# Rounding of the hidden activations moved from ScalarE to VectorE, w2 load issue moved, and the two weight quantisations merged, in a pre-norm transformer block with a ternary-weight FFN

## The reference

```python
def act_quant(x):
    scale = 127.0 / jnp.clip(jnp.max(jnp.abs(x), axis=-1, keepdims=True), 1e-05)
    return jnp.clip(jnp.round(x * scale), -128, 127) / scale
def weight_quant(w):
    scale = 1.0 / jnp.clip(jnp.mean(jnp.abs(w)), 1e-05)
    return jnp.clip(jnp.round(w * scale), -1, 1) / scale
# bit_linear(x, w) = act_quant(x) @ weight_quant(w).T
h = bit_linear(x, w1)                      # 1024 -> 4096
h = depthwise_conv1d(h, conv_w, conv_b)    # 3 taps along the sequence
h = silu(h)
return bit_linear(h, w2)                   # 4096 -> 1024
x = x + attn(layernorm(x)); x = x + ffn(layernorm(x))
```

## Time and profile before

| | us |
|---|---|
| time, median of 2 runs | 4887.63 (4877.98 to 4897.29) |
| the profiled execution | 4897.44 |
| its span on the slowest core (core 2) | 4895.9 |
| spans of the eight cores | 4848.8 to 4895.9 |
| PE busy | 2891.8 (59%) |
| DVE busy | 1615.2 (33%) |
| ACT busy | 1370.4 (28%) |

### The profile page before, as it was taken

One profiled execution on the slowest core, in us unless ns is written; L12 is line 12 of the kernel. 1 busy time (PEld: TensorE's weight loads), 2 busy tenths in 40 slices (PEclk: granted clock), 3 DMA queues, 4 the chain that ended last, 5 costly groups with the idle time before them and its releaser, 6 DMA issues. The chain is left out here.

```text
span 4895.9 us, 49561 instructions; the slowest of 8 cores (4848.8 to 4895.9 us)
## 1 busy us (share of the span) xinstructions
PE 2891.8 (59%) x17394; PEld 1464.8 (30%) x17576; DVE 1615.2 (33%) x3705; ACT 1370.4 (28%) x1640; POOL 45.5 (1%) x68
## 2 busy tenths in 40 slices
PE   0166557778411156767675466467778266677775
PEld 0022123334211134434341122133434143343341
DVE  1121143322233555443432212232111554443431
ACT  0011024457211223232313011024656223140412
POOL 0000000000000000000000000000000000000000
PEclk9999756665655578989777799666565698877878
DMA  7400022111435023435343300000000034434334
GB/s 135 154 22 18 17 95 78 61 61 44 110 97 187 28 53 90 134 105 149 95 125 114 118 22 13 18 27 14 5 18 1 9 69 103 143 101 124 109 108 140
DMA packets 472113, 380.93 MB, mean 78 GB/s; under 512 B 340674, under 2 KB 373570, under 8 KB 466756
## 3 DMA queue, kind: packets, MB, share of 16 engines
q1 hardware_dynamic: 460612, 335.81, 24.2%
q0 software_dynamic: 11264, 41.95, 2.6%
HBM read 335.77 MB, written 41.94 MB: 77 GB/s over the span
## 5 line engine op out<-in xcount | busy, mean ns | idle before, releaser
L80 ACT ACTIVATE b_pt<-b_lp,b_cb 128x1024 bf16<-128x1024 f32 (+3 forms) x640 | 621.4, 985 | 557.0 <-PE b_lp L80 354.8
L80 PE MATMUL c_op<-c_w2b,c_hq 128*128 128x512 bf16 x2032 | 578.8, 435 | 306.6 <-DMA c_w2b<-w2t_s 125.7
L80 PE MATMUL c_hp<-c_xq,c_w1b 128*128 128x257 bf16 x4096 | 550.7, 293 | 117.2 <-ACT c_H L80 108.5
L80 PEld LDWEIGHTS c_hp<-c_xq,c_w1b 128*128 128x128 bf16 x4096 | 420.4, 104 | 285.4 <-issue 192.5
L80 PE MATMUL b_av<-V,b_pt 128*128 128x65 bf16 x5120 | 377.4, 237 | 207.0 <-ACT b_pt L80 146.5
L80 PEld LDWEIGHTS b_av<-V,b_pt 128*128 128x128 bf16 x5120 | 297.0, 124 | 422.0 <-issue 421.9
L80 ACT ACTIVATE c_H<-c_hp,c_cb 128x512 bf16<-128x512 f32 x256 | 175.0, 684 | 824.4 <-DVE c_H L80 531.3
L80 PEld LDWEIGHTS c_op<-c_w2b,c_hq 128*128 128x128 bf16 x2048 | 209.1, 107 | 648.4 <-issue 522.4
L80 PE MATMUL b_lp<-Q,K 64*128 64x512 bf16 x1280 | 371.0, 591 | 11.0 <-DVE x L80 9.3
L80 DVE TENSOR_TENSOR c_H<-c_hp,c_g1b 128x514 bf16<-128x514 f32 x256 | 177.0, 691 | 578.1 <-PE c_hp L80 578.1
L80 DVE MEMSET b_pt<- 128x256 bf16 (+2 forms) x192 | 93.1, 485 | 622.8 <-PE b_lp L80 570.5
(11 more groups left out here) (125 smaller groups left out, 2451.0 us busy)
## 6 DMA issues: line engine op xcount, KB each, us to landing
c_w2b<-w2t_s SPq DMA_DIRECT2D x256, 512.0 KB, 5.4
c_w1b<-w1t_s SPq DMA_DIRECT2D x128, 512.0 KB, 4.6
pw_stg<-w SPq DMA_DIRECT2D x32, 1024.0 KB, 4.9
wq_stw<-w SPq DMA_DIRECT2D x16, 2048.0 KB, 9.0
a_xt<-x SPq DMA_DIRECT2D x32, 512.0 KB, 3.5
b_xr<-x SPq DMA_DIRECT2D x32, 512.0 KB, 3.6
out<-c_obf POOLq DMA_DIRECT2D x32, 512.0 KB, 3.0
wq_s<-p_wbf POOLq DMA_DIRECT2D x16, 512.0 KB, 7.3
```

The source lines that it names most:

```text
L80: h = getattr(eng, en["name"])(*en["args"], **en["kwargs"])
```

## The change

It has four parts.

1. `wprep_quant` becomes `wprep_quant_all`: one loop over 16 blocks, 8 of w1 and then 8 of w2, through the same buffers. The barrier between the two weights is gone, and so is the fresh start of the pipeline.
2. `emit_hq_batch`: both additions of the rounding constant are one DVE `tensor_scalar` (two additions, from c_t, out as bfloat16) instead of two ACT activations. DVE drains after each pair of multiplies and each pair of roundings. Waits on ACT go; PE waits for DVE instead of ACT before a w2 sub; the SiLU into Hb2 waits for the rounding and no longer for the multiply; in front of the batch between tiles it is DVE that waits for the last w2 sub of the previous tile.
3. The batch of a group is recorded earlier: behind the first w2 sub of the group and before w1 chunk 2g+1, where it stood behind `emit_mx`.
4. The w2 load is recorded inside `emit_w2_sub`, right before the sub, where both loads stood at the head of the group.

```diff
-            for blk in range(8):
-                par = blk % 2
+            for j16 in range(16):
+                which = "w1" if j16 < 8 else "w2"
+                t_w = t_w1 if j16 < 8 else t_w2
+                sw_bc = sw1_bc if j16 < 8 else sw2_bc
+                blk = j16 % 8
+                par = j16 % 2
...
-            wprep_quant(t_w1, sw1_bc, mw1_bc, "w1")
-            wprep_quant(t_w2, sw2_bc, mw2_bc, "w2")
+            wprep_quant_all()
...
             def emit_w2_sub(t, half, glob):
                 vp = 0 if half == 0 else 2
                 wb2 = glob % 2
                 g2c = 2 * glob
+                r.wait(r.sync, tn, w2b_cons[wb2])
+                dlw = dw2[wb2].inc(r.sync.dma_start(
...
-                r.wait(r.tensor, sc, ve_hq[2 * glob + 1])
-                r.wait(r.tensor, dw2[wb2], dl_w2[wb2])
+                r.wait(r.tensor, ve, ve_hq[2 * glob + 1])
+                r.wait(r.tensor, dw2[wb2], dlw)
...
-                r.wait(r.scalar, ve, ve_hqm[hc])
+                r.wait(r.scalar, ve, ve_hq[hc])
...
                 r.wait(r.vector, sc, sc_sil[c0 + 3])
-                r.wait(r.vector, sc, ve_hq[(c0 + 31) % 32])
                 for pair in range(2):
-                    if pair == 1:
-                        r.wait(r.vector, sc, ve_hq[c0 + 1])
-                    mv_h = 0
                     for k in range(2):
                         c = c0 + 2 * pair + k
-                        mv_h = ve.inc(r.vector.tensor_mul(
+                        ve.inc(r.vector.tensor_mul(
                             ct1[:, k * 512:(k + 1) * 512],
                             Hb2[:, c * 512:(c + 1) * 512], S2sb[:, :]))
-                        ve_hqm[c] = mv_h
-                    r.wait(r.scalar, ve, mv_h)
+                    ve.inc(r.vector.drain())
                     for k in range(2):
                         c = c0 + 2 * pair + k
-                        sc.inc(r.scalar.activation(
-                            ct1[:, k * 512:(k + 1) * 512],
-                            ct1[:, k * 512:(k + 1) * 512],
-                            AF.Identity, bias=magic_bc[:, 0:1]))
-                    sc.inc(r.scalar.drain())
-                    for k in range(2):
-                        c = c0 + 2 * pair + k
-                        ve_hq[c] = sc.inc(r.scalar.activation(
+                        ve_hq[c] = ve.inc(r.vector.tensor_scalar(
                             hqg[:, c * 512:(c + 1) * 512],
                             ct1[:, k * 512:(k + 1) * 512],
-                            AF.Identity, bias=nmagic_bc[:, 0:1]))
+                            MAGIC, -MAGIC, ALU.add, ALU.add))
+                    ve.inc(r.vector.drain())
...
-                    if w2t is not None:
-                        emit_w2_load(2 * (g % 8))
-                        emit_w2_load(2 * (g % 8) + 1)
                     dg_build(2 * g + 1)
...
                     if w2t is not None:
                         emit_w2_sub(w2t, g // 8, 2 * (g % 8))
+                        if g <= 6:
+                            emit_hq_batch(w2t, 4 * (g + 1))
                     w1_chunk(2 * g + 1, sl)
...
-                    if w2t is not None and g <= 6:
-                        emit_hq_batch(w2t, 4 * (g + 1))
...
                 if t > 0:
-                    r.wait(r.scalar, tn, w2_done[t - 1])
+                    r.wait(r.vector, tn, w2_done[t - 1])
                 emit_hq_batch(t, 0)
```

More of the change, by code:

```diff
@@ L248, in build_program, with wprep_quant_all @@
         r.emit()
[L250 to L256, removed]
+    def wprep_quant_all():
+        with nc.sbuf_tensor("wq_st", [128, 2 * 4096], F32) as stg2, \
+             nc.sbuf_tensor("wq_f", [128, 4096], F32) as qf, \
+             nc.sbuf_tensor("wq_b", [128, 4096], BF16) as qb8, \
+             nc.sbuf_tensor("wq_sp", [128, 4096], BF16) as strip, \
+             nc.psum_tensor("wq_tp", [128, 1024], BF16) as tpp:
             ve_q = 0
@@ L260, in wprep_quant @@
             sc_q = [0, 0]
-            for blk in range(8):
-                par = blk % 2
+            for j16 in range(16):
[4 more added lines that the diff above has]
+                par = j16 % 2
                 stg = stg2[:, par * 4096:(par + 1) * 4096]
-                if blk >= 2:
+                if j16 >= 2:
                     r.wait(r.sync, sc, sc_q[par])
                 if which == "w1":
-                    src = t_w.rearrange("(hc p) (fc f) -> fc p hc f",
-                                        p=128, f=128)[blk]
+                    src_w = t_w.rearrange("(hc p) (fc f) -> fc p hc f",
+                                          p=128, f=128)[blk]
                     dlx[par].inc(r.sync.dma_start(
                         out=stg.rearrange("p (hc f) -> p hc f", hc=32),
-                        in_=src), 16)
+                        in_=src_w), 16)
                 else:
-                    src = t_w.rearrange("(oc p) (hg hq) -> hg p oc hq",
-                                        p=128, hq=512)[blk]
+                    src_w = t_w.rearrange("(oc p) (hg hq) -> hg p oc hq",
+                                          p=128, hq=512)[blk]
                     dlx[par].inc(r.sync.dma_start(
                         out=stg.rearrange("p (oc hq) -> p oc hq", oc=8),
-                        in_=src), 16)
+                        in_=src_w), 16)
                 r.wait(r.scalar, dlx[par])
-                if blk > 0:
+                if j16 > 0:
                     r.wait(r.scalar, ve, ve_q)
@@ L292, in wprep_quant @@
                 for g in range(4):
-                    if not (blk == 0 and g == 0):
+                    if not (j16 == 0 and g == 0):
                         r.wait(r.tensor, ve, ve_g)
@@ L296, in wprep_quant @@
                         if which == "w1":
-                            src_t = qb8[:, (g * 8 + k) * 128:(g * 8 + k + 1) * 128]
+                            src_t = qb8[:, (g * 8 + k) * 128:
+                                        (g * 8 + k + 1) * 128]
                         else:
@@ L947, in build_program @@
             ve_hq = [0] * 32
-            ve_hqm = [0] * 32
             tn_cv = [0] * 32
@@ L960, in build_program @@
             w2b_cons = [0, 0]
[L962 to L971, removed]
             def emit_w2_sub(t, half, glob):
@@ L976, in emit_w2_sub @@
                 g2c = 2 * glob
+                r.wait(r.sync, tn, w2b_cons[wb2])
+                dlw = dw2[wb2].inc(r.sync.dma_start(
+                    out=w2b[:, wb2 * 2048:(wb2 + 1) * 2048].rearrange(
+                        "p (l m) -> p l m", l=2),
+                    in_=t_w2t[g2c:g2c + 2].rearrange("l p m -> p l m")), 16)
                 if glob == 0:
                     r.wait(r.tensor, ve, ve_ev)
-                r.wait(r.tensor, sc, ve_hq[2 * glob + 1])
-                r.wait(r.tensor, dw2[wb2], dl_w2[wb2])
+                r.wait(r.tensor, ve, ve_hq[2 * glob + 1])
+                r.wait(r.tensor, dw2[wb2], dlw)
                 for l in range(2):
```

## The result

| | before | after |
|---|---|---|
| median us (runs) | 4888.01 (10) | 4694.36 (11) |
| lowest to highest | 4874.43 to 4916.69 | 4672.41 to 4739.97 |
| profiled execution | 4897.44 | 4739.97 |
| ratio, 95% interval | | 0.9612 (0.958 to 0.9643) |

A forecast was written before the change was run, and what follows sets the result against it. ACT's queue and the DVE-ACT ping-pong were taken to pace early groups. Savings of 14 (weights), 95 (early groups), 44 (tails) and 6 (between tiles) sum to 159 us, 4738 from 4897.4; forecast 4735, range 4685 to 4800.

The forecast's parts named there:

- fast rival: Stage C: all early groups run at 10.18 us, saving 209 us in all, to 4688 us; chance 0.15.
- What paces early groups: Stage C groups with a rounding batch: ACT's queue and DVE-ACT ping-pong set the pace, 13.63 us a group, not throughput.
- Price of a batch: Rounding on DVE: 0.43 us each, 2.4 us a pair of chunks, 4.7 us a batch, bounds 2.6 to 5.7.
- Where the stall goes: Early groups in stage C: PE next waits for the w2 load, so they take the late groups' pace, 11.36 us.
- Size of the early groups' term: Stage C: 42 early groups go from 13.63 to 11.36 us, 95 us saved, bounds 24 to 145.
- Tail: First-half tail subs go from 4.25 to 2.90 us apart; 22 us a tail, 44 for two.
- Between tiles: At tile changes the first rounded pair is ready sooner: 1 us each for six, 6 us saved.
- Weights: Merged w1 and w2 quantisation: w2's first clip follows w1's last by 21.6 us instead of 35.5, 14 us saved once.
- Cover: Early groups: the DVE batch is hidden behind a group's PE work, 9.3 us, with about 1.8 us to spare.
- slow loads: Rival: later loads or a lower clock hold early groups at 13.05 us; gain 88 us, 4809 us; chance 0.15.
- the rival that had it fall: Low clock throughout: early groups run at the lower clock level, 18.6 us each, 5042 us, slower; chance 0.02.
- H late: Rival: batch costs 5.7 us or more, H(2g+1) passes conv 2g+1's start, groups take 12.5 us; 4786 us; chance 0.05.

The follow-up runs named there:

- batch_at_end: The changed kernel with the rounding batch put back behind the maximum step at the group's end, rounding still on DVE: 4692.03 us, ratio 0.9619 to the kernel before.
- act_early: The changed kernel with rounding back on ACT but recorded at the new, early place: 4901.81 us, ratio 1.0043 to the kernel before.
- before_prefetch: The kernel before with each w2 load recorded behind the sub that frees its buffer: 4834.95 us, ratio 0.9867.
- prefetch_tail5: The changed kernel with each w2 load behind the sub freeing its buffer, and three w1 buffers lent to the tail: 4506.84 us, ratio 0.92 to the kernel before.
- w2_prefetch: The changed kernel with each w2 load recorded behind the sub that frees its buffer: 4563.84 us, ratio 0.9346 to the kernel before.
- the two repetition runs: The changed kernel with each pair of roundings and its drain done two or four times: 4729.83 and 4947.19 us, ratios 0.9672 and 1.0124 to the kernel before.

## Why the prediction was right, point by point

The forecast was 4735 us in a range of 4685 to 4800, faster with 0.83; measured were 4694, inside it, but 41 us under the forecast and 9 above the range's end. That is close to the fast rival's 4688, and by chance: its condition, all early groups at 10.18 us, didn't come (10.83). The gain lay between the two, and the base of the measurement is 9 us under the profiled execution that both started from.

- *What paces early groups.* Right. The DVE-ACT ping-pong and ACT's queue: batch_at_end keeps the gain, act_early loses all of it, before_prefetch turns the load waits into ACT waits. How much is the queue's and how much the ping-pong's stays open.
- *Price of a batch.* Right: the rounding at 128x512 took 0.426 us (0.43 worked out), a pair 2.38 us in prefetch_tail5's tail (2.4), a batch 4.5 (4.7).
- *Where the stall goes.* Right: to the w2 load, 125.7 to 198.1 us, and early groups took the late pace. w2_prefetch removes that wait, and with it 2 us a group.
- *Size of the early groups' term.* 95 us forecast, 42 x (13.60 - 10.83) = 116 measured. The step that was mis-sized is the late pace: I read it from one core, 11.36 us, and that was the slowest of eight, whose mean is 10.91 (10.50 to 11.36). The same working with the mean gives 113. The pace holds the clock's share too, which I hadn't named: 30 us of PE's busy time on the slowest core went with the stalls.
- *Tail.* 44 us forecast, 2 x (71.25 - 49.78) = 43 measured; subs 3.00 us apart, 2.90 forecast.
- *Between tiles.* 6 forecast, 6 x 1.47 = 9 measured.
- *Weights.* 14 forecast, 14.1 in the clips.
- *w2 load moved.* 0, as forecast: SP's streams of the two kernels differ in nothing in stage C.
- *Cover.* Right in kind, and the working had a fault: I took 9.3 us of PE work for a group by adding merged rows of the timeline, whose durations overlap. With PE busy throughout a group is 8.32 us. Since the pace was 10.8, it didn't matter; the two repetition runs put the end of the cover near 2 us more of DVE work, since nearly all beyond that was paid. The forecast's 1.8 us was worked out at 10.18 us a group; at 10.8 the same working gives 2.4.

Sum: 116 + 43 + 9 + 14 = 182 us and a few from group 8 and the late groups (2 x 3 x 0.16 + 24 x 0.12 = 4): 186, beside 183 between the mean spans of the profiled executions and 194 between the medians. The remaining 8 us lie within the interval (175 to 205 us). The forecast's 159 met the difference of the two profiled spans, 157.5, by chance: the early term was 21 us short and the profiled execution of the changed kernel was a long one.

Of the rivals, slow loads did not come, although early windows moved 132 to 152 GB/s instead of 113 to 119. The clock did not fall in early groups (0.83 to 0.93 before, 0.87 to 0.98 after); the rival that had it fall also took 18.6 us for a group's PE work, twice 9.3, where the rows it names, 3.40 against 1.89, give 1.8 times. H late did not come: PE waited 0.8 us for H in all. The fast one (10.18 us a group) was approached: 10.54 to 10.70 on die 1.

## What to carry to other kernels

When an engine in the middle of a chain shares an in-order queue with another chain's work, price the move of that work by what stood behind it, not by its busy time; ACT was 28% busy and still set the pace. A stretch of the same loop without the suspect, here the late groups, gives the new pace in advance, if it is averaged over all cores. After the change, look at what the next wait stands behind in its own queue: one line's place on SP was worth 2.8% once the outer stall was gone, and 1.3% before.

## What the runs showed of the hardware

The granted clock of 0.81 is a level of its own, below full and above the half: in w2_prefetch's profile each core of die 0 ran the late groups of one tile of the second sequence (the second with w2 subs on cores 0 and 1, the third on cores 2 and 3) at 10.0 us each, all others at 8.32, as die 1 did throughout; 10.0/8.32 is 1.20, 1/0.81 is 1.23. The level agrees with the limiter in the Trainium skill (TensorE: Matmul & The Clock Gate, Part 1), which takes a whole die to 13/16 once three of its cores run dense matmuls and holds it while the load lasts. That it lasts with the load these runs don't bear out: PE was as busy in the late groups that ran at 1.00, and prefetch_tail5, with the same groups, had 8.32 us on all eight cores in its profiled execution. Counted from each core's own start, the two stretches at 0.81 in w2_prefetch began 176 us later on cores 2 and 3 than on cores 0 and 1; whether the cores started that far apart or the die wasn't held as one isn't shown. What starts and ends the level isn't settled by these runs.

A shorter wait can be worth more than its length: a chunk behind 3.97 us of PE idling took 3.19 us instead of 1.95 (act_early).
